# Three reductions moved by a part of a convolution or a pair of products: where the statistics of the next layer are formed in a four-layer network

## The chip, the cores and the metric

The kernel runs on one core of a Trainium2 chip, in one launch. The metric is the device time in microseconds from start to end. The kernel before takes 4553.46 us, the median of three runs (4548.0 to 4560.74).

## The reference

The input x has the shape (64, 16, 128, 128): 64 images with 16 channels of 128 x 128 each. There are four layers, each of the form x = x + layer(gn(x)), where gn is a group normalisation over 8 groups of two channels:

```python
def _gn(v, G=8, eps=1e-5):
    g = v.reshape(B_, G, C_ // G, H_, W_)
    m = jnp.mean(g, axis=(2, 3, 4), keepdims=True)
    s = jnp.var(g, axis=(2, 3, 4), keepdims=True)
    return ((g - m) / jnp.sqrt(s + eps)).reshape(v.shape)

x = x + newton_schulz(gn(x), 5)       # layer 0
x = x + conv3x3_quantised(gn(x))      # layer 1: scale by max|gn(x)| over all images, round, 3x3, scale, bias
x = x + conv_diagonal5(gn(x))         # layer 2: 5 taps on the diagonal
x = x + conv3x3_circular(gn(x))       # layer 3: by FFT, so with wrapped edges
```

Layer 0 treats each of the 1024 channel planes as a 128 x 128 matrix W and computes an approximate inverse:

```python
absW = jnp.abs(W)
norm1 = jnp.max(jnp.sum(absW, axis=-2), axis=-1)
norminf = jnp.max(jnp.sum(absW, axis=-1), axis=-1)
X = jnp.swapaxes(W, -1, -2) / (norm1 * norminf)
for _ in range(5):
    X = X @ (2 I - W @ X)
```

## The kernel before, in words

There are two stages with a full stop between them, because layer 1 needs the largest normalised value over all images. Stage A does layer 0 and the statistics of layer 1, stage B does layers 1 to 3. Every engine has its own hand-written program, and the engines meet only at semaphores. Each engine runs its own instructions strictly in the order written, so the place of a call inside a step function is the place of its work.

**Stage A** takes one image per step (64 steps; 62 of them in the full pattern). TensorE ("PE") runs four rounds of products, `products(i, odd, k, p)` with k = 0 to 3 and p = 0 to 7. One call is a pair of matrices; in the trace it is 4 records of L756. Then come the last products (L766). ScalarE ("ACT") copies each pair from PSUM to SBUF (L361), GpSimd ("POOL") forms 2I minus it (L286), and that feeds the next round. Woven between them is the preparation of image i+1 and the statistics of image i-1 (for layer 1) and of image i+2 (for layer 0). The two norms of each matrix of image i+1 are made so: VectorE ("DVE") sums rows and columns; `norm_transpose` (PE, L735) turns the 32 sums; DVE takes the maximum over them and puts it on a diagonal (`norms`: nmax L478, ndiag L480); `norm_broadcast` (PE, L740) multiplies the diagonal by ones so that all partitions see it; DVE's `scale` (L489 to L495) forms the scale from it. On DVE, `norms` stands behind `deviations(1, i - 1)`, whose second instruction is nm (L426). DVE's order after that is four `bn_stats` for image i+2 (L408), `scale`, four more `bn_stats`. PE's `mean(0, i + 2)` (L692) waits for the last of these.

**Stage B** has steps s = 0 to 65. In step s PE convolves image s in layer 1 (`conv(1, ...)`), image s-1 in layer 2 and image s-2 in layer 3. Each convolution has BPI = 4 quarters, u = 0 to 3; one quarter fills one of the six PSUM banks in the ring (128 x 512). A quarter is 3 matmuls and 1 for the halo in layer 1, 15 and 3 in layer 2, 9 and 3 in layer 3 (the records are L1163 for the body and L1170 for the halo). DVE adds each quarter to x (`residual`, L1031 or L1037) and takes its partial statistics (`chunk_stats`, L1048). When all four are there, the group statistics of the next layer follow: `whole_stats` (DVE, L1052), `mean` (PE, L1176, a tiny matmul that mixes partitions), `deviations` (DVE, L1059 to L1070; its second instruction dv<-bs,m is L1061), `var` (PE, L1181), `variance` (DVE, L1074), `root` (ACT, L978), `normalise` (DVE, five small instructions L1083 to L1091 and F<-x,m,r, L1093). After it ACT makes the upper half of the f16 pair (`upper`, L973), POOL the lower half (`lower`, L937), and ACT and SyncE ("SP") issue the DMAs that copy the halo rows (`halos`, L955 and L902), which the next step's convolution reads.

In a steady step the statistics for layer 2 of image s (`mean(2)`, `var(2)`, `normalise(2)`) are formed while PE convolves layer 2 of image s-1, and those for layer 3 of image s-1 while PE convolves layer 3 of image s-2. `quantise` (DVE, three passes L1014, L1017, L1019) prepares layer 1 of image s+1 in the same step. PE waits for nothing but semaphores: a `mean` or `var` whose input is late holds every convolution behind it.

`between` is a function that `conv` calls after its second tap, that is after 6 of the body's 15 matmuls (layer 2) or 6 of 9 (layer 3):

```python
if between and k == 1:
    between()
```

## Time and profile before

| what | value |
|---|---|
| runs of the kernel before | 4560.74, 4553.46, 4548.0 us |
| time of the profiled execution | 4556.31 us |
| its span, first to last instruction | 4554.5 us |
| PE busy | 4378.0 us (96%) |
| DVE busy | 3841.3 us (84%) |
| POOL busy | 2606.1 us (57%) |
| ACT busy | 2249.5 us (49%) |
| mean granted clock of TensorE | 0.99 |

The profiled execution lies 1.8 us above its span, and 2.85 us above the median of the runs. Stage A fills the first 2.5 ms of the span and stage B the rest. PE is busy nearly all the time in both, so what counts is where it waits, and for whom. The rows of the section further down show that. In the timelines, consecutive instructions of one line are one row. A row of several matmuls ends a little after the next row begins, since matmuls are pipelined.

### The profile page before, as it was taken

What the parts mean: (1) busy time and instruction counts of PE and PEld (TensorE: products, weight loads), DVE (VectorE), ACT (ScalarE), POOL (GpSimd) and SP (SyncE); (2) the same over time, 40 slices, a digit from 0 to 9 for tenths busy, and PEclk for the clock granted to TensorE, in tenths of its full rate; (3) what the DMA queues carried; (4) which work ended last, traced back from release to release, by engine and by line L of the source; (5) the groups of instructions that cost most, each with busy time, mean ns of one, the idle gap of its engine ahead of it and who ended that gap; (6) DMA issues with size and microseconds to landing.
All of it is one profiled execution on the core that took longest, in us unless ns stands there. A gap on an engine that the chain in (4) does not pass through costs nothing. (4 is left out here: it accounts for less than half of the span.)

```text
span 4554.5 us, 69799 instructions
## 1 busy us (share of the span) xinstructions
PE 4378.0 (96%) x24265; PEld 3031.8 (67%) x24265; DVE 3841.3 (84%) x8224; ACT 2249.5 (49%) x4551; POOL 2606.1 (57%) x2957
## 2 busy tenths in 40 slices
PE   6999999999999999999997799999999999999998
PEld 6888888888888888888886344444444444444443
DVE  7999999999999999999995777777877877877774
ACT  4777777777777777777775222222222222222221
POOL 7888888888888888888885222222222222222221
PEclk9999999999999999999998899999999999999999
DMA  1111111111111111111111455555555555555553
GB/s 56 58 56 58 55 60 54 55 56 56 56 56 56 56 57 56 56 57 57 57 56 44 103 134 134 133 131 131 138 129 133 137 128 133 138 129 131 138 132 84
DMA packets 333608, 403.52 MB, mean 89 GB/s; under 512 B 23088, under 2 KB 286032, under 8 KB 316880
## 3 DMA queue, kind: packets, MB, share of 16 engines
q1 hardware_dynamic: 308688, 334.25, 29.5%
q10 hardware_dynamic: 24576, 64.79, 5.5%
q8 instruction: 202, 3.31, 0.3%
q14 instruction: 142, 1.16, 0.1%
HBM read 135.22 MB, written 134.22 MB: 59 GB/s over the span
## 5 line engine op out<-in xcount | busy, mean ns | idle before, releaser
L286 POOL TENSOR_TENSOR M<-two,YX 128x256 f32<-128x256 f32 x2560 | 1823.0, 738 | 341.6 <-ACT YX L361 317.1
L756 PE MATMUL bank<-YX,M 128*128 128x256 f32 x8192 | 1930.5, 384 | 0.0
L1163 PE MATMUL bank<-xn,wt 128*128 128x512 f16 (+1 forms) x6912 | 1660.7, 381 | 25.1 <-DVE xn L1019 17.5
L756 PEld LDWEIGHTS bank<-YX,M 128*128 128x128 f32 x8192 | 1494.5, 190 | 179.7
L361 ACT ACTIVATE YX<-bank 128x512 f32<-128x512 f32 x2048 | 1226.7, 599 | 632.2 <-PE bank L756 626.2
L937 POOL TENSOR_TENSOR xn<-F,xn 128x2048 f16<-128x2048 f32 x128 | 487.5, 3809 | 1574.1 <-ACT xn L973 1574.1
L1163 PEld LDWEIGHTS bank<-xn,wt 128*128 128x128 f16 (+1 forms) x6912 | 672.9, 100 | 810.8 <-issue 20.1
L1037 DVE SCALAR_TENSOR_TENSOR x<-bank,wu,x 128x512 f32<-128x512 f32 x512 | 382.3, 747 | 338.7 <-PE bank L1170 329.8
L1170 PE MATMUL bank<-xh,wth 96*128 96x512 f16 (+1 forms) x1792 | 516.2, 381 | 11.2 <-DMA xh<-xn 11.2
L973 ACT ACTIVATE xn<-F 128x2048 f16<-128x2048 f32 x128 | 244.8, 1912 | 566.5 <-DVE F L1093 566.5
L978 ACT ACTIVATE sd<-ve 128x1 f32<-128x1 f32 x128 | 25.9, 203 | 716.5 <-DVE ve L1074 391.4
L408 DVE BATCH_NORM_STATS2 st<-X 128x6 f32<-128x256 f32 x1024 | 367.5, 410 | 9.6 <-DMA X<-in_x 9.5
L469 DVE TENSOR_SCALAR W<-X,m,r 128x256 f32<-128x256 f32 x512 | 373.3, 798 | 2.3
L1048 DVE BATCH_NORM_STATS2 bs<-x 128x6 f32<-128x512 f32 x512 | 355.6, 694 | 17.7
L1170 PEld LDWEIGHTS bank<-xh,wth 96*128 96x128 f16 (+1 forms) x1792 | 174.4, 97 | 231.5 <-DMA xh<-xn 14.0
L352 ACT ACTIVATE YX<-bank,cs 128x128 f32<-128x128 f32 x1024 | 317.0, 388 | 10.7 <-DVE cout L495 10.0
L526 DVE SCALAR_TENSOR_TENSOR X<-bank,cout,X 128x128 f32<-128x128 f32 x1024 | 270.5, 344 | 40.7 <-PE bank L766 40.7
L280 POOL TENSOR_TENSOR W<-W 128x512 f16<-128x512 f32 x256 | 297.9, 1164 | 7.0 <-ACT W L330 7.0
L337 ACT ACTIVATE AD<-X,nm 128x256 f32<-128x256 f32 x512 | 256.7, 503 | 29.8 <-DVE nm L426 29.6
L766 PE MATMUL bank<-YX,M 128*128 128x128 f32 x2048 | 250.1, 280 | 0.0
L766 PEld LDWEIGHTS bank<-YX,M 128*128 128x128 f32 x2048 | 238.4, 192 | 3.1
L727 PE MATMUL bank<-W 128*128 128x128 f16 x3072 | 215.2, 220 | 2.3 <-ACT YX L352 2.3
(107 smaller groups left out, 3582.9 us busy)
## 6 DMA issues: line engine op xcount, KB each, us to landing
X<-in_x SPq DMA_DIRECT2D x64, 1024.0 KB, 4.8
x_scratch<-X SPq DMA_DIRECT2D x64, 1024.0 KB, 5.4
x<-x_scratch SPq DMA_DIRECT2D x64, 1024.0 KB, 8.3
out<-x SPq DMA_DIRECT2D x64, 1024.0 KB, 3.8
xh<-xn SPq DMA_DIRECT2D x384, 131.8 KB, 4.5
xh<-xn ACTq DMA_DIRECT2D x384, 131.8 KB, 5.4
xh<-xn SPq DMA_DIRECT2D x192, 65.9 KB, 2.4
xh<-xn ACTq DMA_DIRECT2D x192, 65.9 KB, 2.4
```

The costliest lines, as they stand in the source:

```text
L286: nc.gpsimd.tensor_tensor(M[odd][:, at, :], two[:, :].unsqueeze(1).broadcast_to([H, 2, H]), YX[odd][:, at, 0:H], ALU.subtract).then_inc(ma ...
L352: ins = nc.scalar.activation(YX[odd][:, mat, 0:H], bank[:, m * H:(m + 1) * H], ACT.Copy, scale=cs[odd][:, mat:mat + 1])
L361: nc.scalar.activation(YX[odd][:, 2 * p:2 * p + 2, :], banks[u % A_RING][:, :].rearrange("p (m w) -> p m w", m=2), ACT.Copy).then_inc(yx_n ...
L408: ins = nc.vector.bn_stats((st0, st1)[k][:, g, :], group_of(X[slot], g))
L469: ins = nc.vector.tensor_scalar(group_of(W, g), group_of(X[slot], g), m0[:, g:g + 1], r0[:, g:g + 1], ALU.subtract, ALU.mult)
L756: ins = nc.tensor.matmul(banks[u % A_RING][:, 2 * H * m:2 * H * (m + 1)], M[odd][:, 2 * p + m, :], YX[odd][:, 2 * p + m, :], start=True, s ...
L766: ins = nc.tensor.matmul(banks[q][:, H * m:H * (m + 1)], M[odd][:, 4 * q + m, :], YX[odd][:, 4 * q + m, H:2 * H], start=True, stop=True)
L937: nc.gpsimd.tensor_tensor(padded(xn[l][odd], 1)[:, 1:NJ + 1, L:L + H], F[l][:, :, :], padded(xn[l][odd], 0)[:, 1:NJ + 1, L:L + H], ALU.sub ...
L1037: nc.vector.scalar_tensor_tensor(out=dst, in0=bank, scalar=wtop[l]["u"][:, 0:1], in1=xs[l][odd][:, a:b, :], op0=ALU.mult, op1=ALU.add).the ...
L1048: nc.vector.bn_stats(bst_[l][:, u, :], xs[l][odd][:, 4 * u:4 * u + 4, :]).then_inc(gchain[l], 1)
L1163: nc.tensor.matmul(bank, wt[l][:, a, k, :], v, start=(k == a == b == 0), stop=False)
L1170: ins = nc.tensor.matmul(bank, wth[l][:, a, :], v, start=False, stop=(a, b) == products[-1])
```

## The change

There are three edits. None adds or removes an instruction; each puts some later or earlier in the order of an engine.

1. Stage A, PE: `norm_broadcast(i + 1)` stood behind `products(i, odd, 1, 7)`. It now stands behind `products(i, odd, 2, 0)`, ahead of `var(1, i - 1)`.
2. Stage B, PE: `var(2)` and `var(3)` stood behind the second quarter (u = 1) of their convolution. They are now issued inside the third quarter (u = 2), after its second tap. `mean` stays inside the second quarter.
3. Stage B, DVE: `variance(2)` moves from ahead of `quantise` to behind it, and `normalise(2)` from the second quarter to the end of the third, behind that quarter's `residual` and `chunk_stats`. `variance(3)` moves from the second quarter to the third, behind its `residual`. `normalise(3)` moves from behind the third quarter's `residual` to just ahead of the fourth's, which is the same place in the order but for `variance(3)`, which now stands directly ahead of it.

```diff
--- before.py
+++ after.py
@@ -781,10 +781,10 @@
                             if prep and p == 5:
                                 norm_transpose(i + 1)
-                            if prep and p == 7:
-                                norm_broadcast(i + 1)
                         for p in range(PAIRS):
                             products(i, odd, 2, p)
+                            if prep and p == 0:
+                                norm_broadcast(i + 1)
                             if post and p == 0:
                                 var(1, i - 1)
@@ -1109,25 +1109,25 @@
                                 if u == 0:
                                     deviations(2, s)
-                                if u == 1:
-                                    variance(2, s)
                             if u == 1:
                                 if there(s + 1):
                                     quantise(s + 1, h + odd, 1 - odd)
                                 if there(s):
-                                    normalise(2, s, odd)
+                                    variance(2, s)
+                            if u == 2 and there(s):
+                                normalise(2, s, odd)
                         if there(s - 1):
                             whole_stats(3, s - 1)
                         for u in range(BPI):
+                            if there(s - 1) and u == 3:
+                                normalise(3, s - 1, prev)
                             if there(s - 2):
                                 residual(3, s - 2, hb, before, u)
                             if there(s - 1):
                                 if u == 0:
                                     deviations(3, s - 1)
-                                if u == 1:
+                                if u == 2:
                                     variance(3, s - 1)
-                                if u == 2:
-                                    normalise(3, s - 1, prev)
@@ -1186,21 +1186,19 @@
+                        between = {1: lambda: mean(2, s), 2: lambda: var(2, s)}
                         if there(s - 1):
                             for u in range(BPI):
                                 conv(2, s, s - 1, h + odd - 1, 1 - odd, u,
-                                     (lambda: mean(2, s)) if u == 1 and there(s) else None)
-                                if there(s) and u == 1:
-                                    var(2, s)
+                                     between.get(u) if there(s) else None)
                         elif there(s):
                             mean(2, s)
                             var(2, s)
+                        between = {1: lambda: mean(3, s - 1), 2: lambda: var(3, s - 1)}
                         if there(s - 2):
                             for u in range(BPI):
                                 conv(3, s, s - 2, h - 1, odd, u,
-                                     (lambda: mean(3, s - 1)) if u == 1 and there(s - 1) else None)
-                                if there(s - 1) and u == 1:
-                                    var(3, s - 1)
+                                     between.get(u) if there(s - 1) else None)
```

The order on PE in stage A, from the transposition of the norms to the mean of image i+2, before (L756 are the products, 2 matmuls of the program to a pair; L735 is norm_transpose, L740 norm_broadcast, L699 var, L692 mean):

```order
L735 MATMUL bank<-idt,absum 32x128
L756 MATMUL bank<-YX,M 128x256 x4
L740 MATMUL bank<-ndiag,ones 128x32
L756 MATMUL bank<-YX,M 128x256 x2
L699 MATMUL bank<-dq,onesv 128x16
L756 MATMUL bank<-YX,M 128x256 x6
L692 MATMUL bank<-st,onesm 128x16
```

and of the changed kernel:

```order
L756 MATMUL bank<-YX,M 128x256 x6
L740 MATMUL bank<-ndiag,ones 128x32
L699 MATMUL bank<-dq,onesv 128x16
L756 MATMUL bank<-YX,M 128x256 x6
L692 MATMUL bank<-st,onesm 128x16
```

The broadcast has moved past one pair; between it and the mean there are now 6 products where there were 8.

The order on PE in the layer 3 convolution of stage B (L1176 is mean, L1181 var), before, from the second quarter on:

```order
L1163 MATMUL bank<-xn_1,wt 128x512 x6
L1176 MATMUL bank<-s,gm 128x1
L1163 MATMUL bank<-xn_1,wt 128x512 x3
L1170 MATMUL bank<-xh_1,wth 128x512 x3
L1181 MATMUL bank<-q,gm 128x1
L1163 MATMUL bank<-xn_1,wt 128x512 x9
L1170 MATMUL bank<-xh_1,wth 128x512 x3
```

and of the changed kernel:

```order
L1176 MATMUL bank<-s,gm 128x1
L1163 MATMUL bank<-xn_1,wt 128x512 x3
L1170 MATMUL bank<-xh_1,wth 128x512 x3
L1163 MATMUL bank<-xn_1,wt 128x512 x6
L1181 MATMUL bank<-q,gm 128x1
L1163 MATMUL bank<-xn_1,wt 128x512 x3
L1170 MATMUL bank<-xh_1,wth 128x512 x3
```

The var has moved past six matmuls of the third quarter.

The order on DVE in the layer 2 convolution of stage B, before, from the partial statistics of the second quarter on (L1074 is variance, L1014 to L1019 quantise, L1083 to L1093 normalise, L1037 residual, bs the partial statistics):

```order
L1048 BN_STATS bs<-x_1 128x6
L1074 TENSOR_SCALAR ve<-bank 128x1
L1014 TENSOR_SCALAR T<-x_1,mcol,acol 128x2048
L1017 TENSOR_SCALAR T<-T 128x2048
L1019 TENSOR_SCALAR xn_1<-T 128x16x128
L1083 RECIPROCAL ra<-sd 128x1
L1085 TENSOR_TENSOR rb<-ra 128x1
L1087 TENSOR_TENSOR rb<-rb,ve 128x1
L1089 TENSOR_SCALAR rb<-rb 128x1
L1091 TENSOR_TENSOR r<-ra,rb 128x1
L1093 TENSOR_SCALAR F<-x_0,m,r 128x2048
L1037 SCALAR_TENSOR_TENSOR x_1<-bank,wu,x_1 128x512
```

and of the changed kernel, from quantise's last pass on:

```order
L1019 TENSOR_SCALAR xn_1<-T 128x16x128
L1074 TENSOR_SCALAR ve<-bank 128x1
L1037 SCALAR_TENSOR_TENSOR x_1<-bank,wu,x_1 128x512
L1048 BN_STATS bs<-x_1 128x6
L1083 RECIPROCAL ra<-sd 128x1
L1085 TENSOR_TENSOR rb<-ra 128x1
L1087 TENSOR_TENSOR rb<-rb,ve 128x1
L1089 TENSOR_SCALAR rb<-rb 128x1
L1091 TENSOR_TENSOR r<-ra,rb 128x1
L1093 TENSOR_SCALAR F<-x_0,m,r 128x2048
```

One residual and one bn_stats (the third quarter's) now stand ahead of the normalisation of layer 2.

## Rows read from the trace of the kernel before

**Rows 1.** Waits of PE: engine, line, waited for, us in total, times, longest.
```profile
PE bank L1181 <- DVE q L1070: 50.0, 63, 3.1
PE bank L740 <- DVE ndiag L480: 24.0, 24, 1.0
```

**Rows 2.** Timeline of PE, stage B, second quarter of layer 3 (start, duration, instruction).
```profile
3426.99 1.47 PE L1163 MATMUL bank<-xn,wt 128*128 128x512 f16 x6
3428.30 0.28 PE L1176 MATMUL bank<-s,gm 128*128 128x1 f32 x2
3428.44 0.82 PE L1163 MATMUL bank<-xn,wt 128*128 128x512 f16 x3
3429.10 0.81 PE L1170 MATMUL bank<-xh,wth 96*128 96x512 f16 x3
3430.67 0.38 PE L1181 MATMUL bank<-q,gm 128*128 128x1 f32 x2 [0.76 <-DVE q L1070]
...
3461.88 0.38 PE L1181 MATMUL bank<-q,gm 128*128 128x1 f32 x2 [0.74 <-DVE q L1070]
```

**Rows 3.** Timeline of DVE around dv<-bs,m of layer 3, a steady step.
```profile
3428.81 1.20 DVE L1061 TENSOR_SCALAR dv<-bs,m 128x8 f32<-128x8 f32 x1
```

**Rows 4.** Timeline of POOL in the same step.
```profile
3426.18 3.81 POOL L937 TENSOR_TENSOR xn<-F,xn 128x2048 f16<-128x2048 f32 x1 [14.86 <-ACT xn L973]
```

**Rows 5.** Timeline of POOL and of DVE in an early step.
```profile
2555.08 3.81 POOL L937 TENSOR_TENSOR xn<-F,xn 128x2048 f16<-128x2048 f32 x1 [22.08 <-ACT xn L973]
...
2556.69 2.23 DVE L1061 TENSOR_SCALAR dv<-bs,m 128x8 f32<-128x8 f32 x1
```

**Rows 6.** Timeline of POOL and PE in the last step with three layers.
```profile
4484.19 3.81 POOL L937 TENSOR_TENSOR xn<-F,xn 128x2048 f16<-128x2048 f32 x1 [11.51 <-ACT xn L973]
...
4491.11 0.33 PE L1181 MATMUL bank<-q,gm 128*128 128x1 f32 x2
```

**Rows 7.** Timeline of DVE, stage B, from the normalisation of layer 2.
```profile
3422.81 1.35 DVE L1093 TENSOR_SCALAR F<-x,m,r 128x2048 f32<-128x2048 f32 x1
3424.07 0.75 DVE L1037 SCALAR_TENSOR_TENSOR x<-bank,wu,x 128x512 f32<-128x512 f32 x1
...
3425.46 0.73 DVE L1037 SCALAR_TENSOR_TENSOR x<-bank,wu,x 128x512 f32<-128x512 f32 x1
```

**Rows 8.** Timeline of ACT after it.
```profile
3424.19 1.91 ACT L973 ACTIVATE xn<-F 128x2048 f16<-128x2048 f32 x1 [5.80 <-DVE F L1093]
```

**Rows 9.** Timeline of PE, stage A, an image with the long wait.
```profile
1317.65 1.89 PE L756 MATMUL bank<-YX,M 128*128 128x256 f32 x8
1320.53 0.40 PE L740 MATMUL bank<-ndiag,ones 32*128 32x32 f32 x2 [0.98 <-DVE ndiag L480]
...
1324.64 0.29 PE L692 MATMUL bank<-st,onesm 128*128 128x16 f32 x2
```

**Rows 10.** Timeline of DVE for the same image.
```profile
1316.13 3.39 DVE L426 TENSOR_SCALAR nm<-mean 128x8 f32<-128x8 f32 x1
...
1322.67 1.40 DVE L408 BATCH_NORM_STATS2 st<-X 128x6 f32<-128x256 f32 x4
```

**Rows 11.** Timeline of POOL for the same image.
```profile
1315.35 4.14 POOL L286 TENSOR_TENSOR M<-two,YX 128x256 f32<-128x256 f32 x6
```

**Rows 12.** Timeline of PE, stage A, the next image, without the long wait.
```profile
1356.15 1.89 PE L756 MATMUL bank<-YX,M 128*128 128x256 f32 x8
1358.08 0.40 PE L740 MATMUL bank<-ndiag,ones 32*128 32x32 f32 x2
1358.42 1.13 PE L756 MATMUL bank<-YX,M 128*128 128x256 f32 x4
...
1362.20 0.29 PE L692 MATMUL bank<-st,onesm 128*128 128x16 f32 x2
```

**Rows 13.** Timeline of DVE for that image.
```profile
1354.62 0.67 DVE L426 TENSOR_SCALAR nm<-mean 128x8 f32<-128x8 f32 x1
...
1360.04 1.40 DVE L408 BATCH_NORM_STATS2 st<-X 128x6 f32<-128x256 f32 x4
```

## The prediction, made before the changed kernel ran

> **What bounds the kernel now.** I read the page first: PE is busy in nearly the whole span, at full clock. So I went on to the list of waits for PE alone. Two of them belong to instructions that the change moves [rows 1]: var (L1181) waits for DVE's q, 63 times and 50.0 us together, and the broadcast of the norms (L740) waits for ndiag, 24 times and 24.0 us. These are the two prizes. Next I read the timelines around each, to see who is really late.
>
> Stage B. A row of matmuls ends 0.16 after the next begins (3428.44 + 0.82 against 3429.10), so PE is through with the second quarter at 3429.10 + 0.81 - 0.16 = 3429.75. The var starts at 3430.67, which is 0.92 lost; the next step's var comes 31.21 later with the same wait [rows 2]. There are about 60 such steady steps. The wait is put down to DVE, but DVE isn't short of time there: its tiny dv<-bs,m takes 1.20 us and ends at 3430.01 [rows 3], and POOL's subtraction (lower(2), L937) ends at 3426.18 + 3.81 = 3429.99 [rows 4]. In an early step the same instruction takes 2.23 and ends at 2558.92; POOL's ends at 2558.89 [rows 5]. In the last step with three layers POOL is done at 4488.00, and the var at 4491.11 waits for nothing [rows 6]. So dv<-bs,m of layer 3 can't run while POOL's subtraction for layer 2 runs; it is let in when that ends, and the var follows 3430.67 - 3429.99 = 0.68 after POOL's end. What PE waits for is POOL.
>
> The Trainium skill, page "SBUF — State Buffer", section "Who interferes with whom", says that VectorE and GpSimd share a pair of SBUF ports as an exclusive lock, that tensor_scalar can be of the kind that needs it, and that the later of the two fully blocks until the first is finished. In these three steps the trace agrees, to 0.03 us [rows 3 to 5]. It speaks against this change, by which POOL's subtraction moves too.
>
> Stage A. With a long wait, PE is through with eight matmuls at 1317.65 + 1.89 - 0.16 = 1319.38, and the broadcast starts at 1320.53: 1.15 lost [rows 9]. DVE's nm, ahead of ndiag on its engine, took 3.39 and ended at 1319.52 [rows 10], POOL's run of six at 1319.49 [rows 11]. In the next image nm takes 0.67 [rows 13] and PE loses 1358.08 - (1356.15 + 1.89 - 0.16) = 0.20 [rows 12]. So of the 62 images of the full pattern 24 have the long wait, and 38 a short one that the list doesn't count.
>
> **Term 1, the var of stage B.** What PE must have done first grows by six matmuls of the third quarter, 3428.30 - 3426.99 = 1.31 [rows 2]. PE gets to the var at 3429.75 + 1.31 = 3431.06 on the clock of that step. If only DVE's own q counted, the wait would be gone. But normalise(2) now stands behind one more residual and bn_stats, 3425.46 - 3424.07 = 1.39 [rows 7]. It gives nothing back, since DVE runs from one to the next without a pause there (F at 3422.81 ends as the residual starts). variance(2) changes only its place ahead of it, and its root on ACT has the residual and bn_stats for cover. From the start of F to POOL's end is 3429.99 - 3422.81 = 7.18, with ACT's copy 3424.19 to 3426.10 between and neither ACT nor POOL pausing for anything else [rows 4, 7, 8]. So F starts at 3424.20, POOL ends at 3431.38, and the var can start at 3432.06. The wait is 3432.06 - 3431.06 = 1.00, where it was 0.92. The deadline moved by 1.31 and its true cause by 1.39. 60 x 0.08 = +5 us. Bounds: the wait gone is -60 x (0.92 + 0.10 for a restart: broadcast 1.13 against half of 1.89 and overlap [rows 12]) = -61; a wait grown by the whole 1.39 is +83. I take +5, since every link has its row.
>
> What is queued behind the blocked dv<-bs,m (now some 2.6 us long, an estimate: from 3428.81 to 3431.40) is q and the residual of the second quarter. Its bank is next needed by layer 1's last quarter in the next step, several us on. var(2), in layer 2's third quarter, finds its q ready as now. DVE's normalise(3) and the fourth residual come about 0.6 later in the step, ahead of residuals that must be ready for mean(2) in the next layer 2: covered by four quarters of layer 1 and one of layer 2. The halo DMAs of ACT and SP for layer 2 follow POOL by the same 1.39, those of ACT for layer 1 follow `upper`; they have until the next step, and no steady step now waits for a DMA. I cost these at nothing. If the cover were gone, each would add up to 1.4 per step. At the very end nothing covers variance(3) and its root ahead of the last normalise(3): two tiny instructions on two engines, which I put at +0.5 (0 to 1).
>
> **Term 2, the broadcast of stage A.** One pair is half of 1.89 - 0.16, that is 0.865 [rows 12]. Without the long wait, PE now comes to the broadcast at 1357.88 + 0.865 = 1358.74, when ndiag has been ready for 0.7. What goes: the 0.20 of waiting; the broadcast's own 1358.42 - 1358.08 = 0.34 becomes the 0.14 that an unstalled small matmul takes (3428.44 - 3428.30 [rows 2]); and the four matmuls behind it restart without loss (1.13 - 0.16 = 0.97 against 0.865), 0.10. Together 0.50. What is late next is mean(0) (L692). It would come at 1362.20 - 0.50 = 1361.70; its bn_stats end at 1360.04 + 1.40 = 1361.44 [rows 12, 13]. That is 0.26 in hand, little once the weights must be fetched first, so I take 0.45. The scale on DVE stands behind four bn_stats, some 1.3 us, and still finds the broadcast done.
>
> With the long wait, the broadcast keeps its time, since it waits for ndiag as before, but PE has done a pair meanwhile. The mean would come at 1324.64 - 0.865 = 1323.78 [rows 9], but its bn_stats end at 1322.67 + 1.40 = 1324.07 [rows 10]. So a new wait at the mean takes about 0.35 back and restarts once more at 0.10: 0.4 saved of 1.15. Sum: 38 x 0.45 + 24 x 0.4 = 17 + 10 = -27 us. Bounds: 0 (the mean takes all back) and -(38 x 0.50 + 24 x (1.15 + 0.20 + 0.10)) = -54. Which images have the long wait I leave as it is: nm and POOL's run are both timed by PE's rounds, which the edit doesn't touch before them.
>
> **Sum.** +5 + 0.5 - 27 = about -21.5 on the profiled execution's 4556.3 us, so 4535. The median of the runs is 2.85 lower, which about three long waits fewer would explain (1.0 us each); in such an execution the gain is the same. 4553.5 - 21.5 = 4532; I forecast 4534.
>
> **The rivals.**
> - *The mean holds everything in stage A* (20%). The reserve of 0.26 isn't enough, for example because weights are asked for ahead of the matmul, and DVE's chain by bn_stats sets the end. Then term 2 is 0 to -5, and the time 4555. For it: in the images with a long wait it does so already. Against it: bn_stats comes first by the rows in the other 38.
> - *No long waits at all* (9%). nm slips in behind POOL's first instruction, always. Term 2 is then -27 less another 24 x 1.0: 4510. By the same page and section of the skill the loser is blocked only until the other's instruction ends. That is what 0.67 is [rows 13], but 3.39 goes past five of them [rows 10, 11]; there the trace disagrees.
> - *The var's wait is gone* (8%), because what blocks dv<-bs,m isn't POOL's end but something that stays at its place. Then term 1 is -61: 4553.5 - 61 - 27 = 4466. The three ends that agree [rows 3 to 5] speak against it.
> - *Slower* (8%): the long wait of nm becomes the rule. One mechanism, in stage A at L426: POOL is fed a little earlier after each image, since PE no longer pauses, and nm meets a POOL run without a gap every time. Each of the 38 turned images costs about 1.05 (1.0 of wait and 0.05 less saved): 4534 + 40 = 4574. It decides from some 20 turned images on. For it: nothing separates the two kinds of image in the timelines. Against it: the phase comes from PE.
>
> **How the numbers follow.** The forecast has 55%, with its own range of 4526 to 4544 (0.1 us per steady step is 6 us, and the number of long waits varies by several). The range that should hold the time 8 times in 10 is 4510 to 4558: it takes in the first two rivals and leaves out the others. A measurement of this kernel can tell 0.3%, or 13.7 us, from no change. Faster than 4539.8 are most of the forecast and the second and third rival: 62%. Within are the first rival and the forecast's upper part: 28%. Slower: 10%.
>
> **What would show it.** In the changed profile, dv<-bs,m of layer 3 should take about 2.6 us and end with POOL's L937; L1181 should still wait for q about 60 times; the step should be 31.3 long. In stage A, L740 should wait hardly at all in most images, L692 should wait for st some 24 times, and images should come 37.1 or 38.1 apart. Term 1 is wrong if the step is 30.2 long, term 2 if images still come 37.5 apart, the count of long waits if it is far from 24.

## The result and the profile after

| | before | after |
|---|---|---|
| median of the runs, us | 4553.37 (10 runs) | 4565.31 (10 runs, 4553.18 to 4568.23) |
| ratio, 95% interval | | 1.0025 [1.0014, 1.0036] |
| profiled execution, span, us | 4556.31, 4554.5 | 4568.23, 4566.4 |
| stage A / stage B, us | 2507.5 / 2047.0 | 2513.9 / 2052.6 |

The changed kernel is slower by 0.25%; forecast was 21.5 us less. Of the 11.9 us between the profiled executions stage A has +6.4 and stage B +5.6. The waits of PE, which answer to [rows 1]:

```profile
PE bank L1181 <- DVE q L1070: 55.3, 63, 4.3
PE bank L692 <- DVE st L408: 38.7, 38, 12.5
PE bank L740 <- DVE ndiag L480: 3.3, 21, 0.2
```

The var of stage B waits as often as before and a little longer. The broadcast hardly waits, but the mean of image i+2 does: 36 times in the full pattern and twice at the start (before: these two alone).

**Stage B.** PE in a steady step, against [rows 2]:

```profile
3406.69 0.28 PE L1176 MATMUL bank<-s,gm 128*128 128x1 f32 x2
3408.14 1.47 PE L1163 MATMUL bank<-xn,wt 128*128 128x512 f16 x6
3410.43 0.38 PE L1181 MATMUL bank<-q,gm 128*128 128x1 f32 x2 [0.82 <-DVE q L1070]
3410.67 0.82 PE L1163 MATMUL bank<-xn,wt 128*128 128x512 f16 x3
...
3441.72 0.38 PE L1181 MATMUL bank<-q,gm 128*128 128x1 f32 x2 [0.82 <-DVE q L1070]
```

DVE and POOL in the same step, against [rows 3, 4]:

```profile
3407.20 2.58 DVE L1061 TENSOR_SCALAR dv<-bs,m 128x8 f32<-128x8 f32 x1
3405.94 3.81 POOL L937 TENSOR_TENSOR xn<-F,xn 128x2048 f16<-128x2048 f32 x1 [15.54 <-ACT xn L973]
```

The six matmuls end at 3408.14 + 1.47 - 0.16 = 3409.45, so 0.98 is lost to the var at 3410.43. The tiny dv<-bs,m is now 2.58 long and ends at 3409.78, POOL at 3409.75. The median step is 31.289 long, before it was 31.217.

**Stage A.** An image with the long wait: PE, against [rows 9],

```profile
1321.89 0.40 PE L740 MATMUL bank<-ndiag,ones 32*128 32x32 f32 x2 [0.15 <-DVE ndiag L480]
1322.22 0.39 PE L699 MATMUL bank<-dq,onesv 128*128 128x16 f32 x2
...
1325.88 0.39 PE L692 MATMUL bank<-st,onesm 128*128 128x16 f32 x2 [0.57 <-DVE st L408]
```

and DVE and POOL for it, against [rows 10, 11]:

```profile
1317.46 3.42 DVE L426 TENSOR_SCALAR nm<-mean 128x8 f32<-128x8 f32 x1
1323.95 0.57 DVE L495 TENSOR_SCALAR cout<-cs 128x16 f32<-128x16 f32 x1
1324.43 1.39 DVE L408 BATCH_NORM_STATS2 st<-X 128x6 f32<-128x256 f32 x4
1316.70 4.16 POOL L286 TENSOR_TENSOR M<-two,YX 128x256 f32<-128x256 f32 x6
1323.76 0.73 POOL L286 TENSOR_TENSOR M<-two,YX 128x256 f32<-128x256 f32 x1 [0.16 <-ACT YX L361]
```

An image without it, against [rows 12], with PE's weight loads (PEld) last:

```profile
1396.00 2.76 PE L756 MATMUL bank<-YX,M 128*128 128x256 f32 x12
1398.69 0.40 PE L740 MATMUL bank<-ndiag,ones 32*128 32x32 f32 x2
1399.02 0.39 PE L699 MATMUL bank<-dq,onesv 128*128 128x16 f32 x2
1399.27 2.84 PE L756 MATMUL bank<-YX,M 128*128 128x256 f32 x12
1401.94 0.29 PE L692 MATMUL bank<-st,onesm 128*128 128x16 f32 x2
1398.69 0.29 PEld L740 LDWEIGHTS bank<-ndiag,ones 32*128 32x128 f32 x2 [0.33 <-issue]
```

For the images of each kind, in us (a short image is one without the long wait of nm, a long image one with it):

| | short, before | short, after | long, before | long, after |
|---|---|---|---|---|
| images of the 62 | 38 | 26 | 24 | 36 |
| start to start of images | 37.550 | 37.440 | 38.50 | 38.504 |
| nm starts to broadcast starts | 3.461 | 4.207 | 4.416 | 4.431 |
| broadcast starts to mean starts | 4.114 | 3.251 | 4.114 | 3.984 |
| wait at L740 / L692 | none listed | none | 1.004 / none | 0.152 / 0.570 |

So a short image saves 0.11 and a long one nothing, and 12 more images are long. The 38 save 38 x 0.11 = 4.2, the 12 cost 12 x 1.06 = 12.7; of the +6.4 some -2 is left over. It lies ahead of the first full image, whose nm starts at 98.14 and before at 100.24; kernels that have the same order there differ by as much.

### The profile page after: what moved, and what is told of

It is laid out like the page before. It is cut to its first block and busy times, and to the rows that moved or that the text cites. A ratio compares the mean times of both kernels' runs of the same rounds, so it can differ in the third digit from the quotient of the medians.

```text
span 4566.4 us, 69799 instructions
## 1 busy us (share of the span) xinstructions
PE 4385.5 (96%) x24265; PEld 3028.9 (66%) x24265; DVE 3951.1 (87%) x8224; ACT 2241.0 (49%) x4551; POOL 2609.7 (57%) x2957
## 5 line engine op out<-in xcount | busy, mean ns | idle before, releaser
L756 PE MATMUL bank<-YX,M 128*128 128x256 f32 x8192 | 1915.5, 383 | 0.0
L1163 PE MATMUL bank<-xn,wt 128*128 128x512 f16 (+1 forms) x6912 | 1679.8, 382 | 25.2 <-DVE xn L1019 17.1
L756 PEld LDWEIGHTS bank<-YX,M 128*128 128x128 f32 x8192 | 1499.8, 190 | 180.4
L1037 DVE SCALAR_TENSOR_TENSOR x<-bank,wu,x 128x512 f32<-128x512 f32 x512 | 382.7, 748 | 219.6 <-PE bank L1170 209.7
```

The costliest lines, as they stand in the source:

```text
L756: ins = nc.tensor.matmul(banks[u % A_RING][:, 2 * H * m:2 * H * (m + 1)], M[odd][:, 2 * p + m, :], YX[odd][:, 2 * p + m, :], start=True, s ...
L1037: nc.vector.scalar_tensor_tensor(out=dst, in0=bank, scalar=wtop[l]["u"][:, 0:1], in1=xs[l][odd][:, a:b, :], op0=ALU.mult, op1=ALU.add).the ...
L1163: nc.tensor.matmul(bank, wt[l][:, a, k, :], v, start=(k == a == b == 0), stop=False)
```

## The experiments

Each comparison was made on one chip, the four on four chips, and each has runs of the kernel before of its own; ratios are against these. "Long images" are those of the 62 in which nm waits for POOL's run, counted in the one profiled execution.

**First comparison (kernel before: 4567.46 us).** The change is cut along its edits.

`bcast_only`, edit 1 alone:

```diff
-                            if prep and p == 7:
-                                norm_broadcast(i + 1)      # behind products(i, odd, 1, p)
+                            if prep and p == 0:
+                                norm_broadcast(i + 1)      # behind products(i, odd, 2, p)
```

> The kernel before with the first edit alone (norm_broadcast one pair of products later in stage A). Theory (the broadcast now stands next to var, its weight load is no longer hidden, the mean(0) behind it waits for bn_stats, and long waits of nm come more often): an image without a long wait 37.44 us apart from the next instead of 37.55, one with a long wait 38.50 as before; some 33 long waits instead of 21; time about 4553.4 + 6 = 4559 to 4560 us, stage B with its 31.2 us steps untouched. Rival (stage A gained what I predicted, and the loss of the changed kernel comes from stage B): 4527 us. Rival (the two parts only lose together): 4553 us.

Measured 4540.87, ratio 0.9942 [0.9929, 0.9956]. Some 33 long images and 4559 were expected. The two kinds of image are as in the changed kernel (37.429 and 38.467), but only 17 are long. PE's waits in it:

```profile
PE bank L692 <- DVE st L408: 27.7, 19, 12.5
```

`stats_only`, edits 2 and 3 alone, the diff of the change without its first hunk:

> The kernel before with the edits of stage B alone (var(2), var(3), variance, normalise). Theory (dv<-bs,m of layer 3 waits for the end of POOL's subtraction for layer 2, which comes 1.39 later, while PE's deadline comes 1.31 later): steps of 31.29 us instead of 31.215, dv<-bs,m 2.58 us long, 60 x 0.075 = +5 us, about 4558.5 us, with some 21 long waits of nm in stage A as before. Rival (the wait of the var is DVE's own lateness and the edits of stage B remove it): 4553 - 60 = 4493 us. Rival (all of the loss is in stage B): 4565 us.

4569.33, ratio 1.0004 [0.9995, 1.0013]; step 31.288, as in the changed kernel, and 36 long images. The first two kernels differ by 28 us, of which 19 images of about 1.0 are the greater part. Until the number of long images is known, a total says little here.

`var3_only`, of edits 2 and 3 only what concerns layer 3:

```diff
+                            if there(s - 1) and u == 3:
+                                normalise(3, s - 1, prev)
...
-                                if u == 1:
+                                if u == 2:
                                     variance(3, s - 1)
-                                if u == 2:
-                                    normalise(3, s - 1, prev)
...
+                        between = {1: lambda: mean(3, s - 1), 2: lambda: var(3, s - 1)}
```

> The kernel before with only layer 3's part of the edits of stage B: var(3) inside the third quarter, variance(3) behind its residual, normalise(3) ahead of the fourth residual; layer 2's statistics stay where they were. Theory (POOL's end sets q of layer 3, and it stays at 25.06 us of the step while PE's deadline moves from 24.8 to 26.1): dv<-bs,m still 1.20 us long and still ending with POOL, but q is ready at 25.7 us and PE no longer waits; steps of 30.2 us instead of 31.215, 60 x 1.0 = -60 us, about 4493 us. Rival (it is the order on DVE around layer 3 that makes q late, which this edit shares with the changed kernel): 31.3 us steps, about 4558 us.

4502.47, ratio 0.9859 [0.9844, 0.9873], the step 30.20, though 36 images are long. Its waits, and DVE, POOL and PE in a step:

```profile
PE bank L1181 <- DVE q L1070: 4.0, 2, 2.9
```

```profile
3412.69 1.20 DVE L1061 TENSOR_SCALAR dv<-bs,m 128x8 f32<-128x8 f32 x1
3410.05 3.81 POOL L937 TENSOR_TENSOR xn<-F,xn 128x2048 f16<-128x2048 f32 x1 [14.37 <-ACT xn L973]
3414.93 0.28 PE L1181 MATMUL bank<-q,gm 128*128 128x1 f32 x2
```

dv<-bs,m is blocked as before and ends with POOL, 3413.89 against 3413.86. The var comes 1.07 after POOL's end, where it was 0.68 behind POOL, and waits for nothing. The later place helps as long as POOL stays where it was.

`norm2_back`, the changed kernel with normalise(2) put back ahead of the third quarter:

```diff
                                 if there(s):
                                     variance(2, s)
-                            if u == 2 and there(s):
-                                normalise(2, s, odd)
+                                    normalise(2, s, odd)
```

> The changed kernel, but with normalise(2) back in the second quarter on DVE, directly behind variance(2) (no residual and bn_stats between them, so the root on ACT is waited for). Theory: POOL's subtraction for layer 2 ends about 25.4 us into the step instead of 26.44, q of layer 3 is ready at about 26.1, just when PE gets there; the wait of 1.0 us goes, steps of 30.2 to 30.3 us, -60 us from the changed kernel: about 4505 us. Rival (not the place of normalise(2) decides): as the changed kernel, 4565 us.

4489.69, ratio 0.9834 [0.9821, 0.9847]; step 30.342, 18 long images. The var (L1180 in this kernel) waits only twice, 4.2 together, and dv<-bs,m is held for 1.63 where it was 2.58. This one line is worth (31.289 - 30.342) x 60 = 57 us: it is what moved POOL and took back the gain of the later var.

**Second comparison (kernel before: 4554.77).**

`after_again`, the changed kernel, no edit:

> The changed kernel once more. Theory: its time is a fixed part and the number of long waits of nm (L426) in stage A, each worth 1.06 us, where each is worth 0.95 us before; that number belongs to the chip or the moment and to the layout of stage A together. With n long waits of 62 the changed kernel takes 4530 + 1.06 n, the kernel before 4533.4 + 0.95 n. If this chip gives the changed kernel some 17 (as the kernel with the first edit alone had) it takes about 4548; with some 36 it takes 4568. Rival (the slowdown of 0.25% is a property of the change): ratio 1.002 to 1.003 to the kernel before on the same chip, whatever the chip.

4563.21, ratio 1.0003 [0.9974, 1.0032], 32 long images: too wide to say anything on the ratio. The time is what was expected for this number, 4530 + 32 x 1.06 = 4564.

`no_nm`, the kernel before without nm; ACT takes -mean as a scale of -1 instead:

```diff
-                            nc.vector.tensor_scalar(nm1[:, :], mean, -1.0, None, ALU.mult).then_inc(neg_mean, 1)
...
-                ACT.Abs, bias=nm1[:, g:g + 1])
+                ACT.Abs, bias=mean1[:, n, g:g + 1], scale=-1.0)
```

> The kernel before without the instruction nm in stage A: ACT takes the absolute deviation as |mean - x| with scale -1 and the mean itself as bias, so its wait is on the mean. Theory (the port race is nm's alone: a tensor_scalar that must find a gap in POOL's run, which comes only because ACT itself waits for nm and so starves POOL): no image with 38.5 us, all at 37.5 us or less: 4533 us or less, and a smaller spread over the runs. Rival (any DVE instruction with two SBUF inputs has the race): dev (L427) now has waits of 3 us or more in a third of the images, longer than before since ACT no longer starves POOL: up to 5.6 us, and the time 4560 us or more.

4583.05, ratio 1.0002 [0.9952, 1.0052], inconclusive as a time, with runs from 4537 to 4649. But the wait has only moved, to the next instruction, dev<-st,mean, which reads two operands from SBUF (ns, least/median/most):

```profile
L425 DVE TENSOR_TENSOR dev<-st,mean x64: 175/669/3424, 98.6 to 2497.8; 128x16 f32<-128x16 f32 x64
```

So nm as such isn't the cause: the next instruction behind the mean that reads SBUF in this way is caught instead. It happens in 17 images, which now take 39.1 or 40.8 where the others take 37.43, so here each costs 1.6 or 3.3 us. One of them on DVE and on POOL:

```profile
324.85 3.42 DVE L425 TENSOR_TENSOR dev<-st,mean 128x16 f32<-128x16 f32 x1
324.06 5.70 POOL L286 TENSOR_TENSOR M<-two,YX 128x256 f32<-128x256 f32 x8
327.48 0.76 POOL L286 TENSOR_TENSOR M<-two,YX 128x256 f32<-128x256 f32 x1
```

ACT has no nm to wait for and feeds POOL on, so POOL's run has eight instructions here. The last row is the sixth of them alone. It ends at 328.24 and dev at 328.27, while POOL goes on until 324.06 + 5.70 = 329.76. In all 17 images dev is let in behind the same instruction, the fifth that it overlaps, with the next one begun. With nm the wait had the same length, 3.42, and POOL's run ended there.

`var1_apart`, edit 1, and var(1) one pair later, so that broadcast and var don't stand side by side:

```diff
-                            if post and p == 0:
+                            if post and p == 1:
                                 var(1, i - 1)
```

> The kernel before with the first edit, and var(1) one pair later too, so that the broadcast and var no longer stand next to each other on PE (order: products(2,0), broadcast, products(2,1), var). Theory (two small f32 matmuls in a row cost 0.33 + 0.25 us because their weight loads, about 0.19 each and two per f32 matmul, have nothing to hide behind): with products between them they cost about 0.14 to 0.2 each; an image without a long wait takes 37.15 to 37.25 us instead of 37.44; 45 such images make -10 us against the kernel with the first edit alone, at the same number of long waits. Rival (the 0.3 us is the restart after a wait or is given back at mean(0), which waits for bn_stats): 37.4 us as with the first edit alone.

4547.43, ratio 0.9973 [0.9941, 1.0005]. Short images are 37.439, against 37.440 with them side by side, and the mean comes 3.251 behind the broadcast in both. Expected was 37.15 to 37.25: the neighbour isn't what costs.

`dv_psum`, the changed kernel, L1061 reads the mean from PSUM:

```diff
-                        link.done(nc.vector.tensor_scalar(dev[l][:, :], means(l)[:, :, 1], c["m"][:, 0:1], None,
-                                                          ALU.subtract))
+                        link.done(nc.vector.tensor_tensor(dev[l][:, :], means(l)[:, :, 1],
+                                                          banks[4 + l][:, 0:1].broadcast_to([H, 2 * BPI]), ALU.subtract))
```

> The changed kernel, with dv<-bs,m (L1061) as a tensor_tensor that reads the mean from PSUM, so that it has one SBUF input. Theory (the port that DVE shares with POOL is what blocks it): this instruction no longer waits, 0.2 us; the next one, dv*dv (L1064), which has two SBUF inputs, waits in its place, about 2.2 us, until POOL's subtraction ends, and the step stays at 31.29 us. Rival (POOL slows or blocks DVE as a whole, or something else about this one instruction): the wait stays on the same instruction, or vanishes and the step is 30.3 us.

One run, 4534.3, with 17 long images. DVE and POOL:

```profile
3412.30 0.17 DVE L1061 TENSOR_TENSOR dv<-bs,bank 128x8 f32<-128x8 f32 x1
3412.49 2.37 DVE L1064 TENSOR_TENSOR dv<-dv 128x8 f32<-128x8 f32 x1
3411.03 3.81 POOL L937 TENSOR_TENSOR xn<-F,xn 128x2048 f16<-128x2048 f32 x1 [15.31 <-ACT xn L973]
```

With the mean read from PSUM the subtraction runs in 0.17 in the middle of POOL's; the square behind it, with both in SBUF, is held until 3414.86 and POOL ends at 3414.84. What matters is where the operands lie. The step was expected to stay at 31.29 and is 31.083. One small instruction less stands behind POOL's end, and the var starts at 3415.32, 0.48 behind it, where it was 0.68.

**Third comparison (kernel before: 4546.26, 27 runs).**

`after_third` and `bcast_again` are the changed kernel and edit 1 alone once more:

> The changed kernel again, on the same chip as the kernel with its first edit alone (bcast_again). Both have the same instructions in stage A. Theory 1 (the number of long waits of nm belongs to the chip and the moment): both have about the same number, so the changed kernel is 4 to 7 us slower (its 60 steps of 31.29 instead of 31.215) and no more. Theory 2 (the number belongs to the build: something outside stage A's order, such as where code lies, differs between the two kernels): the changed kernel has 30 to 36 long waits on every chip and the other about 17, so the changed kernel is 20 to 26 us slower.

> The kernel with the first edit alone again, on the same chip as after_third. Theory 1 (chip and moment): as many long waits as after_third on this chip. Theory 2 (build): about 17 long waits and 4540 us again, whatever the kernel before and the changed kernel take here.

4552.58, ratio 1.0014 [1.0005, 1.0023], with 23 long images; and 4550.58, ratio 1.0011 [1.0002, 1.002], with 21. The same programs had 36 and 17 before and lay 24 us apart in their medians; here they lie 2 us apart. So the number of long images isn't fixed by the program, and the 27 us of `bcast_only` are no gain that the edit gives everywhere.

It isn't shown that the place of the broadcast has no part in that number. In the first comparison the two kernels with the old place had 36 and 36 long images (`stats_only`, `var3_only`), the two with the new place 17 and 18 (`bcast_only`, `norm2_back`). In this one the kernels with the new place have 21, 23 and, in `full_rows`, 26, and the kernel before about 13, an estimate from 24 at 4556.31 us, its median of 4546.26 here and 0.95 us for each. On one chip the later place goes with half the long images, on another with more, as in the main result. Why is open.

`port_free_a`, the kernel before with stage A's small chain through PSUM, so that no instruction from the mean to ndiag has two SBUF operands or is of the tensor_scalar kind on SBUF:

```diff
+                        mp = banks[6 + k][:, 320:320 + G]
+                        dp = banks[6 + k][:, 336:336 + 2 * G].rearrange("p (g a) -> p g a", a=2)
...
-                            nc.vector.tensor_scalar(nm1[:, :], mean, -1.0, None, ALU.mult).then_inc(neg_mean, 1)
...
-nc.vector.tensor_scalar(ndiag[:, :], idt[0:2 * C, 0:2 * C], nmax[:, 0:1], None, ALU.mult)
+nc.vector.tensor_tensor(ndiag[:, :], idt[0:2 * C, 0:2 * C],
+                        banks[6][0:2 * C, 400:401].broadcast_to([2 * C, 2 * C]), ALU.mult)
```

> The kernel before, with the chain of stage A from mean to ndiag made so that no instruction needs the port that DVE shares with POOL: nm is gone (ACT takes |mean - x| with scale -1), and mean, deviation, its square and the maximum go through PSUM, so that each instruction has at most one SBUF input and none is a tensor_scalar from SBUF to SBUF; one small instruction more. Theory (only the fight for that port makes the long waits, and PE waits for ndiag only through them): no image 38.5 us, every image at 37.43 us, 62 x 0.12 us and all long waits less: 4526 us, the runs within 5 us of each other. Rival (the race is about semaphores or POOL's own timing): images of 38.5 us remain, 4540 us or more.

4522.62 (4521.15 to 4524.86), ratio 0.9948 [0.9936, 0.9961]. All images take 37.42 to 37.45: the long wait is gone, and with it most of the spread of the times. Two rows of its waits:

```profile
PE bank L1183 <- DVE q L1072: 49.8, 63, 2.9
PE bank L694 <- DVE st L408: 18.0, 2, 12.4
```

`full_rows`, edit 1 with the broadcast's matmul over all 128 rows (ndiag padded with zeros):

```diff
-                ndiag = sb("ndiag", [2 * C, 2 * C])
+                ndiag = sb("ndiag", [H, 2 * C])      # rows 32 on set to 0 once
...
-                ones[0:2 * C, :], ndiag[:, :]
+                ones[:, :], ndiag[:, :]
```

> The kernel with the first edit alone, with the broadcast over all 128 rows (ndiag padded with zeros to 128 partitions) instead of 32. Theory (a matmul on 32 rows of the array can't have its weights loaded ahead of 128-row matmuls, nor they behind it: it costs 0.09 + 0.33 us even when nothing is waited for, and that is what I took for the price of the wait): the weight load of L740 now starts before the matmul ahead of it ends, the broadcast costs 0.14 us, an image without a long wait takes 37.15 us instead of 37.44, and one with a long wait 38.4 to 38.5 as before: 45 x 0.29 = 13 us less than bcast_again at the same number of long waits. Rival (any small f32 matmul at that place costs this): no difference.

4542.6, ratio 0.9992 [0.9983, 1.0001], with 26 long images. Short images take 37.225, 0.20 less than in `bcast_again` beside it (37.427), and the mean comes 3.037 behind the broadcast. Expected was 37.15. PE and its weight load:

```profile
1080.26 0.30 PE L742 MATMUL bank<-ndiag,ones 128*128 128x32 f32 x2
1080.40 0.37 PE L701 MATMUL bank<-dq,onesv 128*128 128x16 f32 x2
1080.05 0.41 PEld L742 LDWEIGHTS bank<-ndiag,ones 128*128 128x128 f32 x2
```

The load now starts 0.21 ahead of its matmul and the next follows after 0.14. With 32 rows (the image at 1398.69 above) the load began with its matmul and the next followed 0.33 later, though DVE had ended ndiag 0.78 ahead of it.

**Fourth comparison (kernel before: 4577.05).**

`after_port_free`, the changed kernel with the edit of `port_free_a`:

> The changed kernel with the port-free chain in stage A. Theory (without the long waits only the sure effects of the change are left: the broadcast's later place is worth nothing once ndiag is early, and stage B loses 0.075 us in each of 60 steps and about 1.5 us at its ends): every image at 37.43 us as in the kernel before with that chain, stage B 6.3 us longer than there: 4522.6 + 6.3 = 4529 us. Rival (the first edit has a gain of its own that the long waits hid): 4522 us or less.

4527.44, ratio 0.9894 [0.9879, 0.9908]. The change is read against `port_free_a`, without long images in either: images 37.44 against 37.43, stage A 2473.1 against 2472.9, stage B 2052.6 against 2046.4. It costs 6.4 us of span, nearly all in stage B. In this form the short images of the old place are at 37.43 too, so edit 1 has nothing left to gain.

`port_free_b`, the kernel before, both SBUF operands of stage B's deviations avoided:

```diff
+                        dp = banks[4 + l][:, 64:64 + 2 * BPI]
+                        qp = banks[4 + l][:, 80:80 + 2 * BPI]
...
-                        link.done(nc.vector.tensor_tensor(dev[l][:, :], dev[l][:, :], dev[l][:, :], ALU.mult))
+                        link.done(nc.vector.tensor_tensor(qp, dp, dev[l][:, :], ALU.mult))
```

> The kernel before with only the deviations of stage B port-free: the deviation is formed once to PSUM and once to SBUF with the mean read from PSUM, its square goes to PSUM, one small instruction more. var, variance and normalise stay where they were. Theory (POOL's subtraction blocks q through the port, and by nothing else): no instruction of the chain waits, q is ready about when PE gets to the var in its old place, steps of 30.2 to 30.35 us, 60 x 0.9 = -54 to -60 us from the kernel before on this chip. Rival (POOL's subtraction delays q in another way): 31.2 us.

4517.62, ratio 0.9866 [0.9848, 0.9884], despite 44 long images; step 30.265, stage B 1990.5. The var (L1185 in this kernel) waits twice, 2.3 together. The wait of [rows 1] is worth 56 us of stage B, and POOL's subtraction causes it.

`all_parts`, `var3_only` with both chains through PSUM and the 128-row broadcast in its old place; `all_parts_e1`, the same with edit 1:

> The parts that helped, together: layer 3's var in the third quarter (var3_only), the port-free chains of both stages, and the broadcast over 128 rows; the broadcast in its old place. Theory (the parts are independent): stage A 2473 - 62 x 0.1 to 0.2 = 2461 to 2467 us, stage B 1987 us, 4450 to 4456 us. Rival (what one part gives, another takes back): 4465 us or more.

> all_parts with the broadcast one pair later, as in the change. Theory (ndiag is early in the port-free chain, so the place of the broadcast costs and gives nothing): within 3 us of all_parts. Rival (bn_stats and mean(0) become late, as in the images with a long wait): 5 to 20 us slower.

4441.65, ratio 0.9704 [0.9689, 0.9718], and 4448.31, ratio 0.9718 [0.9704, 0.9733]. The first beats both kernels, with images of 37.12 and steps of 30.20, and is below the 4450 to 4456 that was expected; the second was expected within 3 us of it and is 6.7 slower. From its page:

```profile
span 4439.4 us, 70121 instructions
PE 4336.0 (98%) x24265; PEld 3036.7 (68%) x24265; DVE 3661.7 (82%) x8544; ACT 2249.0 (51%) x4551; POOL 2604.8 (59%) x2958
```

Edit 1 makes images 37.22 there: with the broadcast over 128 rows, which waits for nothing in its old place, moving it costs 0.10 per image. Over 32 rows it costs nothing (37.43 and 37.44, `port_free_a` and `after_port_free`). Why isn't shown; the mean doesn't wait in either, as the rival had it. That the broadcast then has the var for a neighbour is one reading, and `var1_apart` speaks against it for the 32-row form.

## Why the prediction was wrong

**Term 1 held.** Its links came out as worked out: dv<-bs,m 2.6 long (2.58), ending with POOL; a wait of 1.00 (0.98); a step longer by 0.08 (0.072). 61 steps gave 4.4, an early step 1.35 more, the two ends of the stage took 0.2 back, together +5.6 against +5.5. The prediction speaks of three ends that agree, but its rows show two; in the whole trace dv<-bs,m is held in 62 steps and ends 0.02 to 0.03 behind POOL in each. `var3_only` moves the deadline alone, `norm2_back` takes back the move of POOL alone, `port_free_b` takes away the conflict alone; each removes it but for the first two of the stage. The rival "the var's wait is gone" was true of every one of these and not of the change, which moves the blocker by more than the deadline.

**The step that failed for a short image** is "Together 0.50". Of 0.20 + 0.20 + 0.10 only some 0.12 was waiting: the broadcast stands 0.746 later behind nm, where a pair is 0.865, and the mean keeps its distance in PE work (4.114 - 3.251 = 0.863, a pair). The rest was read as a stall and is, in part at least, the price of this matmul. I compared its 0.34 with the 0.14 of a 128-row one [rows 2, 12], but it has 32 rows, and takes 0.33 with ndiag long ready too. `full_rows` gets 0.20 back, by another edit; that is half of the 0.39 by which 0.50 was too high. The other half, the wait and the restart read too high, no run takes apart. The reserve of 0.26 at the mean, on which the first rival hung, was never used: L692 doesn't wait in short images. Term 2 came out near that rival's "0 to -5" all the same, by another mechanism.

**The step that failed for a long image** is "a new wait at the mean takes about 0.35 back". It is 0.57, and 0.15 remain at the broadcast. The two times of bn_stats were taken as fixed, but cout, just ahead of them, went from 0.17 to 0.57: POOL's single M, 1323.76 + 0.73 = 1324.49, now falls on it, and cout ends at 1324.52. It is 0.55 to 0.57 in all 36 long images. That it is the same conflict as at nm is read from these ends, and no run took it alone.

**The third** is "Which images have the long wait I leave as it is". 36 came instead of 24, as in the rival on the slow side, whose price per image (1.05) was right (1.06), whose place (L426) was right, and whose reason (POOL fed earlier, so nm always meets a full run) no run bears out: in the first comparison the kernels with the new place had fewer long images. The profiles with the broadcast in its old place show 24, 36, 36 and 44 long images, those with it in the new one 36, 32, 23, 17, 21, 18, 35, 17 and 26: the two overlap from 24 to 36. The kernel before, with medians from 4546 to 4577 in the five sets of its runs, moves more than the change does. Whether the edit, the chip or both made 36 out of 24 stays open.

**The sum at one count.** With n long images in both, the change costs +5.6 in stage B and saves (62 - n) x 0.11 + 2 in stage A: -0.6 at n = 24, against -21.5. Without the 2, which may be chance, it is +1.4. `stats_only` and the changed kernel differ by edit 1 alone and have 36 long images each; their stage A takes 2517.8 and 2513.9, 3.9 less, where the sum gives 4.9. Worked with what was measured, stage A's term is -6, and not -27. The measured 1.0025 is that plus the unlike counts, and with stage A's chain through PSUM the change costs 6.4 us, or 0.14%.

**What stays open** is what decides whether nm slips in. It starts 60 to 120 ns after one of POOL's instructions in both kinds of image, with the run going on in both; the short ones end with the instruction that runs, the long ones four further, at the last of a run of six. One might think that DVE is let in because the run ends, and that the run ends because ACT, which feeds POOL, comes to wait for nm. `no_nm` speaks against it: there ACT feeds POOL on, and dev is let in after the same 3.42 in the middle of the run. So the end of the run isn't what ends the wait, and what does is not shown.

The Trainium skill, page "SBUF — State Buffer", section "Who interferes with whom", has the loser of the port blocked until the other's instruction ends. For the single long POOL instruction of stage B all ends agree within 0.03 us. For nm behind back-to-back instructions of 0.7 it doesn't hold: 3.42 lasts until the fifth that it overlaps has ended, and by the rule there would be no long image.

## What to carry to other kernels

A wait goes away only if the edit moves the deadline by more than it moves what really blocks; find the blocker by equal ends of instructions, not by the engine named. Before a gap beside an instruction is booked as waiting, look for the same form of instruction when nothing waits. Where times of one kernel spread by 0.5%, count the event with two lengths in each profile first, and where the trace shows two engines blocking each other, consider both cures: moving an operand of the tiny instructions to PSUM gave 56 us in stage B and, in stage A, 24 us by the medians of one chip, and the one new place in the order that left the blocker where it was (`var3_only`) gave 60 in stage B.

## What the runs showed of the hardware

- The 32-row f32 matmul of the broadcast takes 0.33 until the next starts, and its load isn't begun ahead; with 128 rows it is 0.14 and the load starts 0.21 ahead. Padding with zeros made an image 0.20 shorter.
- A DVE instruction of 8 or 16 elements a partition was held up to 3.4 us in stage A for POOL, and up to 2.6 in a steady step of stage B (3.4 and 3.6 in single early steps of the changed kernel). It happened to tensor_scalar on SBUF and to tensor_tensor with both inputs in SBUF, and not once to the instructions with an input in PSUM, which took 0.29 at most.
- The 3.42 for which nm or dev is held behind POOL's short instructions is the same whether POOL's run ends there or goes on.
- The number of images in which this happens, 17 to 44 of 62, differs from program to program and, for one program, from chip to chip. Each costs 1.0 us, and 1.6 or 3.3 without nm.
